# Twelve-head attention of a language-model tower: from turns of two halves to phases over three pairs, with biases as a 97th weight row

## Chip, core and metric

One NeuronCore of one Trainium2 chip. The metric is the device time of the kernel in microseconds (us). A core has five engines that run side by side and meet at semaphores: TensorE (PE; its weight loads are PEld), VectorE (DVE), ScalarE (ACT), GpSimd (POOL) and SyncE (SP).

## What is computed

4096 tokens (32 rows of 128) of width 192 go through an embedding and five blocks. The change is in the fourth: a transformer layer's attention with twelve heads of 16 (over the 128 tokens of a row), and the routing for the mixture of experts that follows. Cut to what matters:

```
qkv  = ln(x) @ in_proj_w.T + in_proj_b          # ln(x) * g + b, width 192
att  = softmax(q @ k.T / 4)  per head, 12 heads, 128 x 128
y    = ln(x) + (att @ v) @ out_proj_w.T + out_proj_b
z    = ln(y)
p    = softmax(ln2(z) @ router_w.T + router_b)  # 8 experts, the best 2 taken
```

The kernel keeps z as rows to send, adds y to its residual, and gives every token two places in the list of rows per expert.

## The kernel before

32 token tiles stay in the SBUF tile resid. The attention block works on **pairs** of tiles (M = 2, 256 tokens), 16 in all; even pairs belong to stream p0 with PSUM banks 0 to 3, odd ones to stream p1 with banks 4 to 7. All engines run the same order, written as generators that `alternate` takes turn by turn; every `yield` is a place where the other generator goes on. `in_turns_routed` (L915) puts `first` of one pair beside `second` of the pair before it in the other stream.

- `first` (`vector_m_1`, `tensor_m_1`, `scalar_m_1`): statistics and normalised rows (DVE L1845 to L1861, the root on POOL L1047), turning (PE L966), features for q and k (24 matmul records at L1007), values (16 at L1000), scores (L1987, 24 records for a tile), row maxima (DVE L1839), which are turned (PE L2036) and put into spare rows of the queries (DVE L1880), scores once more with keys and queries exchanged (L1987), exponentials (ACT L2107), the product with the values (PE L2000).
- `second` (`vector_m_2` and so on): turned back (PE L2008), division (DVE L1888, L1889), turning (L966), output projection (L1000), sum and statistics (DVE L1893, L1019 to L1024), root (POOL L1047), rows of the router (DVE L1030), residual (DVE L1898), turning, router logits (PE L2066).
- `picked` and `placed` run inside the `first` of the stream's next pair: the two best experts by 11 small dependent DVE instructions, running counts, positions by two matmuls (PE L2074, L2075), row numbers; `send` (POOL L1973, L1977) scatters the rows.

An fp32 matmul stands in the profile as two records. `ch.step(ins)` makes DVE wait for its own instruction before the next. The biases of values, output projection and router are added by DVE (L1870, L1861, L1900) from tiles that hold them on all 128 partitions.

Of the kernel before, what the change touches and what calls it, by code (L numbers as in the profile page):

```python
# [16 lines left out]
P = 128  # L17
# [78 lines left out]
def tower(nc, a, out):  # L96

    with ExitStack() as ctx:
# [687 lines left out]
        m_rb, m_rank = W.take(E), W.take(G * E)  # L786
        mb_v, mb_o, mb_qk = W.take(D), W.take(D), W.take(6)
# [51 lines left out]
        for dst, name in ((lw_1b, "L1_attn_w1"), (lw_2b, "L1_attn_w2")):  # L839
# [5 lines left out]
            (mw_r[0:C], halves("L1_ffn_router_w")), (m_rb, rows("L1_ffn_router_b")), (m_rank, AP["rank"]),  # L845
            (mb_v, AP["L1_ffn_in_proj_b"][2 * D:3 * D].partition_broadcast(P)), (mb_o, rows("L1_ffn_out_proj_b")),
# [69 lines left out]
        def in_turns_routed(eng, first, second, routed, over=lambda: None, at_start=lambda: ()):  # L916

            p0, p1 = streams
            alternate(first(0, p0, False), iter(at_start()))
            over()  # L920
            alternate(first(0, p1, False), second(0, p0, False))
            alternate(first(1, p0, True), second(0, p1, False))
# [5 lines left out]
            alternate(first(NG - 1, p1, True), second(NG - 1, p0, True))  # L928
            alternate(second(NG - 1, p1, True), routed(NG, p0))
            over()  # L930
            alternate(routed(NG, p1))
            over()
# [382 lines left out]
        def pool_rest(pool):  # L1315
# [7 lines left out]
            in_turns_routed(pool, lambda g, a, prev: pool_m_1(pool, g, a, m_signals(a), prev),  # L1323
                            lambda g, a, prev: pool_m_2(pool, g, a, m_signals(a), prev),
                            lambda g, a: pool_routed(pool, g, a, m_signals(a)), at_start=lambda: pool_m_pads(pool))
            pool_x(pool)

        def tensor_rest(pe):
# [10 lines left out]
            in_turns_routed(pe, lambda g, a, prev: tensor_m_1(pe, g, a, m_signals(a), prev),  # L1339
                            lambda g, a, prev: tensor_m_2(pe, g, a, m_signals(a), prev),  # L1340
                            lambda g, a: tensor_routed(pe, g, a, m_signals(a)))
            tensor_x(pe)

        def scalar_rest(act):
# [10 lines left out]
            in_turns_routed(act, lambda g, a, prev: scalar_m_1(act, g, a, m_signals(a), prev),  # L1355
                            lambda g, a, prev: scalar_m_2(act, g, a, m_signals(a), prev),
                            lambda g, a: scalar_routed(act, g, a, m_signals(a)))
# [101 lines left out]
        def pool_m_pads(pool):  # L1459

            yield
# [8 lines left out]

        def vector_m_padded(v):

            v.wait_ge(s_pad, 6)
            yield
# [327 lines left out]
        for a in streams:  # L1802
# [4 lines left out]
            a.m_den = take(M * H, M)  # L1807

# [11 lines left out]
        def m_signals(a):  # L1820

            s = Own()
            s.var, s.root, s.x, s.xT_p, s.xT, s.qk_p, s.qk, s.v_p, s.v, s.scores, s.rowmax, s.top_p, s.topped, \
                s.scoresT, s.exp, s.oT_p, s.oT, s.pv_p, s.out, s.T2_p, s.T2, s.proj_p, s.ffn_in, s.T3_p, s.T3, \
                s.router_p, s.r_lg, s.r_eg, s.r_sel, s.r_pos_p, s.r_pos, s.r_dst = a.sems[0:32]
            return s

        def vector_m(v, ch):
            in_turns_routed(v, lambda g, a, prev: vector_m_1(v, ch, g, a, m_signals(a), prev),
                            lambda g, a, prev: vector_m_2(v, ch, g, a, m_signals(a), prev),  # L1830
# [11 lines left out]
        def vector_m_1(v, ch, g, a, f, prev):  # L1842

            for i in range(M):
                ins = nc.vector.bn_stats(a.st[:, i, :], tiles_of(g, a)[:, i, :])  # L1845
# [660 lines left out]
```

## Time and profile before

| | |
|---|---|
| median of 3 runs | 2083.55 us (2078.67 to 2085.76) |
| the profiled execution, span | 2106.3 us |
| its attention block (DVE's first instruction at 1217.2 to the next block's first turned rows at 1718.1) | 501 us |
| mean granted TensorE clock, whole span | 0.822 |
| PE, DVE, ACT, POOL busy | 77%, 62%, 46%, 19% of the span |

The page gives one profiled execution. Its first part sums each engine's busy time over the whole span; its second cuts the span into 40 slices of 52.7 us, of which slices 24 to 32 are the attention block. The granted clock has two levels, 0.5 (1.2 GHz) and 1.0 (2.4 GHz); a digit in between is a mix over time.

### The profile page before, as it was taken

How to read it: one execution, taken by the hardware profiler on the slowest of the kernel's cores; microseconds unless marked ns; L12 is line 12 of the kernel's file. 1: busy time of each engine (PE TensorE's matmuls, PEld its weight loads, DVE VectorE, ACT ScalarE, POOL GpSimd, SP SyncE). 2: the span in 40 equal slices, each digit the busy share in tenths (PEclk: the TensorE clock that was granted, in tenths of full speed). 3: DMA queues.
4: the chain of work that ended last, by engine and by line, in shares of the span. 5: the costliest groups of instructions: out<-in, count | busy, mean ns of one | idle time of the engine just before them, and what ended most of it. 6: DMA issues, size and time to landing. Idle time of an engine off the chain costs nothing.

```text
span 2106.3 us, 35471 instructions
## 1 busy us (share of the span) xinstructions
PE 1611.5 (77%) x12060; PEld 1159.8 (55%) x12060; DVE 1312.3 (62%) x4361; ACT 979.3 (46%) x2773; POOL 400.4 (19%) x494
## 2 busy tenths in 40 slices
PE   0166764968888578888888768888888759999996
PEld 0032223855665355555555456666676647777775
DVE  7898885878888677877788536555555532122221
ACT  1366998933444445554555323333333324443442
POOL 7302331000000100000000001222212223333332
PEclk9975555578888689999999878777777769999998
DMA  3000001079910000000000000000000037777775
GB/s 71 15 1 1 1 1 20 3 141 193 188 20 0 1 1 0 0 0 0 0 0 0 1 25 13 24 23 23 23 15 19 23 96 179 185 175 181 177 176 133
DMA packets 136262, 112.99 MB, mean 54 GB/s; under 512 B 29417, under 2 KB 128457, under 8 KB 136137
## 3 DMA queue, kind: packets, MB, share of 16 engines
q1 hardware_dynamic: 119320, 91.70, 18.4%
q0 software_dynamic: 16864, 20.33, 5.0%
q8 instruction: 40, 0.66, 0.1%
q14 instruction: 38, 0.30, 0.1%
HBM read 69.19 MB, written 45.94 MB: 55 GB/s over the span
## 4 chain that ended last, share of the span: by engine, by line
PE 52%; DVE 27%; ACT 14%; issue 4%; POOL 1%; DVEq 0%; DMA 0%; another core or an unknown queue 0%; SPq 0%; ACTq 0%; POOLq 0%
ACT bank L716 8%; PE bank L2322 8%; PE bank L1007 6%; PE bank L2307 5%; PE bank L2311 3%; PE bank L1987 3%; PE bank L966 3%; PE bank L1217 2%; PE bank L1665 2%; PE bank L1000 2%; PE bank L2000 2%; DVE WK L1839 1%; DVE WK L1581 1%; DVE R L1581 1%; DVE R L1839 1%
## 5 line engine op out<-in xcount | busy, mean ns | idle before, releaser
L1047 POOL TENSOR_TENSOR WK<-WK,mhalf 128x2 f32<-128x2 f32 (+1 forms) x96 | 77.9, 812 | 882.4 <-DVE WK L1505 328.4
L2359 ACT ACTIVATE R<-bank,R 128x256 f32<-128x256 f32 x234 | 98.2, 471 | 216.9 <-PE bank L2311 216.9
L2211 DVE SCALAR_TENSOR_TENSOR WK<-bank,R,WK 128x192 f32<-128x192 f32 x78 | 28.9, 413 | 262.8 <-PE bank L2322 262.8
L716 ACT ACTIVATE bank<-bank,nbias,sc 128x128 f32<-128x128 f32 x384 | 168.9, 991 | 22.6 <-POOL nbias L528 22.6
L1007 PE MATMUL bank<-WK,R 96*128 96x256 f32 x576 | 162.9, 429 | 17.0 <-ACT WK L973 11.0
L2240 POOL DMA_INDIRECT moe_sum<-WK x78 | 121.5, 1557 | 257.4 <-DVE WK L2211 196.4
L2322 PE MATMUL bank<-R 128*128 128x192 f32 x936 | 169.1, 331 | 0.0
L716 ACT ACTIVATION_READ_ACCUMULATOR bank<-bank,nbias,sc 128x1 f32 x384 | 163.0, 766 | 0.0
L2322 PEld LDWEIGHTS bank<-R 128*128 128x128 f32 x936 | 150.1, 190 | 13.3 <-issue 13.3
L1007 PEld LDWEIGHTS bank<-WK,R 96*128 96x128 f32 x576 | 116.2, 213 | 41.9 <-ACT WK L973 15.4
L2307 PE MATMUL bank<-R 128*128 128x256 f32 x468 | 125.2, 390 | 1.1 <-ACT R L2350 1.1
L1987 PE MATMUL bank<-WK 32*128 32x128 f32 x1536 | 84.4, 367 | 35.4 <-DVE R L1839 13.0
L610 PE MATMUL bank<-R 32*128 32x128 bf16 x384 | 62.7, 299 | 60.0 <-ACT bank L716 57.1
L966 PE MATMUL bank<-ident,WK 128*96 128x128 f32 x320 | 66.4, 345 | 44.3 <-DVE WK L1030 27.7
L1987 PEld LDWEIGHTS bank<-WK 32*128 32x128 f32 x1536 | 69.2, 255 | 50.5 <-DVE R L1839 15.3
L2307 PEld LDWEIGHTS bank<-R 128*128 128x128 f32 x468 | 84.0, 191 | 20.9 <-issue 13.3
L610 PEld LDWEIGHTS bank<-R 32*128 32x128 bf16 x384 | 29.4, 118 | 118.7 <-ACT bank L716 106.6
L1665 PE MATMUL bank<-WK,R 128*128 128x256 f32 x256 | 75.6, 420 | 15.0 <-ACT WK L993 15.0
L433 DVE TENSOR_REDUCE neg_all<-bank 128x3 f32<-128x384 f32 x128 | 69.4, 554 | 27.4 <-PE bank L610 25.2
L559 PE MATMUL bank<-R,wq 96*128 96x512 bf16 x192 | 79.3, 542 | 4.6 <-DVE WK L407 2.7
L2311 PE MATMUL bank<-R 64*128 64x256 f32 x468 | 82.7, 430 | 0.0
L1000 PE MATMUL bank<-R,WK 96*128 96x192 f32 x384 | 76.4, 343 | 2.9 <-ACT WK L973 1.4
(494 smaller groups left out, 3886.4 us busy)
## 6 DMA issues: line engine op xcount, KB each, us to landing
moe_rows_in<-zeros SPq DMA_DIRECT2D x1, 25026.0 KB, 138.7
R<-in_L_ffn_w SPq DMA_DIRECT2D x39, 576.0 KB
R<-in_L_ffn_w SPq DMA_DIRECT2D x39, 384.0 KB
R<-moe_rows_in SPq DMA_DIRECT2D x39, 194.0 KB, 4.6
R<-in_L_ffn_w SPq DMA_DIRECT2D x78, 96.0 KB
R<-in_L_ffn_b SPq DMA_DIRECT2D x39, 96.0 KB
moe_sum<-resid POOLq DMA_DIRECT2D x16, 192.0 KB
moe_sum<-WK POOLq DMA_INDIRECT x78, 5.9
```

The source lines that it names most:

```text
L610: mm = nc.tensor.matmul(bank[u % 4][:, k * P:(k + 1) * P], qk[32 * j:32 * j + 32, k, i * P:(i + 1) * P], qk[32 * j:32 * j + 32, 3 + k, i * ...
L716: ins = nc.scalar.activation(s, s, ACT.Exp, bias=nbias[:, u, k:k + 1], scale=col(SS), accum_out=units(sum_all, g, u)[:, k:k + 1])
L966: mm = nc.tensor.transpose(a.bank[b][0:C, c * NM + i * P:c * NM + (i + 1) * P], src[:, i, c * C:(c + 1) * C], ident[:, :])
L1000: mm = nc.tensor.matmul(a.bank[b][:, i * D:(i + 1) * D], a.xT[0:C, c, i * P:(i + 1) * P], w[0:C, c, :], start=(c == 0), stop=(c == 1))
L1007: mm = nc.tensor.matmul(out, w[0:C, c, m], a.xT[0:C, c, :], start=(c == 0), stop=(c == 1))
L1665: nc.tensor.matmul(a.bank[c][:, out], wa[:, c * P:(c + 1) * P], a.xT[:, 0, :], start=True, stop=False)
L1987: mm = nc.tensor.matmul(a.bank[j][:, k * P:(k + 1) * P], x, y, start=True, stop=True)
L2240: pool.indirect_dma_start(out=acc, out_offset=bass.IndirectOffsetOnAxis(ap=x_id[k % B3][:, t:t + 1].bitcast(U32), axis=0), in_=x_y[k % B3] ...
L2307: nc.tensor.matmul(bank[b + n][:, 0:NR], xw_1a[h][:, q * P:(q + 1) * P], x_T[h][:, 0, :], start=True, stop=False)
L2311: mm = nc.tensor.matmul(bank[b + n][:, 0:NR], xw_1b[h][s, p * P:(p + 1) * P], x_T[h][s, 1, :], start=False, stop=True)
L2322: mm = nc.tensor.matmul(bank[4 + t][:, 0:D], x_hid[f][:, t * P:(t + 1) * P], xw_2[h][:, f, :], start=(p == 0 and n == 0), stop=(p == PAIRS ...
L2359: ins = nc.scalar.activation(x_hid[q], bank[(0, 2, 0)[p] + n][:, 0:NR], ACT.Gelu, bias=xb_1[h][:, q:q + 1])
```

## The change

- `in_phases` takes the place of `in_turns_routed`. A phase works on up to five things: S, the pair whose scores are made; T, the pair before it, from its product with the values to its normalised rows; N, the pair after it, turned and multiplied to q, k and v (in T's stream); L, the pair two after S, whose statistics and normalised rows are made; R, the pair two before S, which is routed. There are 16 phases with an S, and two more that empty the line.
- PE's, DVE's, ACT's and POOL's orders inside a phase are written out. On DVE `weave` puts an instruction of a filler (the picking of R, the statistics of L) behind each of the main one; `mark` and `need` wait for a step only where its result is used.
- The biases of values, output projection and router are row 97 of the weights (partition 96), against a row of ones in `xT` and in a new tile `m_tT`. DVE's three additions go; ACT copies the values out of PSUM (`take_values`) and makes the base of the sum (`base`). T's turned rows go to `m_tT` and no longer over `xT`.
- N's features use banks 0 and 1 of T's stream, T's and R's turned rows bank 2, projection and logits bank 3.
- POOL's memsets (`pool_m_pads`) stand ahead of its first root, and DVE waits for them before its first statistics.

```diff
-            alternate(first(0, p0, False), iter(at_start()))
...
+            phase((0, p0), None, (0, p1), (1, p0), None)
+            phase((0, p1), (0, p0), (1, p0), (1, p1), None)
             over()
             with eng.Fori(1, NG - 1) as g:
-                alternate(first(g, p1, True), second(g, p0, True))
-                alternate(first(g + 1, p0, True), second(g, p1, True))
+                phase((g, p0), (g - 1, p1), (g, p1), (g + 1, p0), (g - 1, p0))
+                phase((g, p1), (g, p0), (g + 1, p0), (g + 1, p1), (g - 1, p1))
                 over()
...
+            phase(None, (NG - 1, p1), None, None, (NG - 1, p0))
+            phase(None, None, None, None, (NG - 1, p1))
...
+            def phase(S, T_, N_, L_, R):
+                r = picked(*R) if R else iter(())
+                l = normed_twice(*L_) if L_ else iter(())
+                if S:
+                    run(row_tops(*S, 0))
+                if R:
+                    run(logits(*R))
+                if S:
+                    weave(row_tops(*S, 1), r)
+                if T_:
+                    weave(divided(*T_), r)
+                if S:
+                    weave(tops_into_queries(*S), r)
+                if T_:
+                    weave(attended(*T_), r, l)
+                run(r)
+                run(l)
+                if T_:
+                    run(routed_rows(*T_))
+                p = placed(*R, other(R[1]).bank[2][:, 0:M * E]) if R else iter(())
+                if L_:
+                    weave(rows_of_pair(*L_), p)
+                run(p)
...
+            def with_bias(x, w, out):
+                for i in range(M):
+                    n = w.shape[2]
+                    nc.tensor.matmul(out[:, i * n:(i + 1) * n], x[0:C + 1, 0, i * P:(i + 1) * P], w[0:C + 1, 0, :],
+                                     start=True, stop=False)
+                    mm = nc.tensor.matmul(out[:, i * n:(i + 1) * n], x[0:C, 1, i * P:(i + 1) * P], w[0:C, 1, :],
+                                          start=False, stop=True)
+                return mm
...
+                if S:
+                    g, a = S
+                    f = m_signals(a)
+                    pe.wait_ge(f.qk, per(g, 4, 4))
+                    scores(g, a, 0, f.scores, False)
+                if R:
+                    gr, c = R
+                    fr = m_signals(c)
+                    if T_:
+                        pe.wait_ge(m_signals(T_[1]).exp, per(T_[0], 4 * M, 8))
+                    pe.wait_ge(fr.ffn_in, per(gr, 2, 1))
+                    turn(other(c), c.xr, 2, fr.T3_p)
+                if T_:
+                    gt, b = T_
+                    ft = m_signals(b)
+                    times_v(*T_, 0)
+                    times_v(*T_, 1)
+                if R:
+                    pe.wait_ge(fr.T3, per(gr, 1, 1))
+                    with_bias(c.m_tT, mw_r, other(c).bank[3]).then_inc(fr.router_p, 1)
+                if S:
+                    pe.wait_ge(f.rowmax, per(g, 4 * M, 4))
+                    scores(g, a, 1, f.scores, False)
+                if N_:
+                    gn, n = N_
+                    fn = m_signals(n)
+                    pe.wait_ge(fn.x, per(gn, 1, 1))
+                    if T_:
+                        pe.wait_ge(ft.oT, per(gt, M, 1))
+                    turn(n, n.hs, 0, fn.xT_p)
...
+                if T_:
+                    pe.wait_ge(ft.out, per(gt, M, M))
+                    turn(b, b.m_ao, 2, ft.T2_p)
+                if S:
+                    tops_turned(*S, 0)
+                    tops_turned(*S, 1)
+                if T_:
+                    pe.wait_ge(ft.T2, per(gt, 1, 1))
+                    with_bias(b.m_tT, mw_o, b.bank[3]).then_inc(ft.proj_p, 1)
+                if N_:
+                    features(n, 0)
+                if S:
+                    pe.wait_ge(f.topped, per(g, M, M))
+                    scores(g, a, 0, f.scoresT, True)
+                if N_:
+                    pe.wait_ge(fn.qk, per(gn, 4, 1))
+                    features(n, 2)
+                    pe.wait_ge(fn.qk, per(gn, 4, 2))
+                    with_bias(n.xT, mw_v, n.bank[0]).then_inc(fn.v_p, 1)
+                if R:
+                    positions(*R, other(c).bank[2][:, 0:M * E])
+                if S:
+                    pe.wait_ge(f.exp, per(g, 4 * M, 4))
+                    scores(g, a, 1, f.scoresT, True)
+                if T_:
+                    pe.wait_ge(ft.var, per(gt, 1, 1))
+                if R:
+                    pe.wait_ge(fr.r_pos, per(gr, 1, 1))
```

How the order of instructions moves, as the two programs issue them (an ISA or REGISTER_ALU row is a wait that stands by itself or an address; counts are instructions). First PE in the loop, from the scores of a pair's first tile to its second scores. Before, with L966 turning, L2036 the turned row maxima, L1000 a product with the values' or the projection's weights and L2066 the router:

```order
L1987 MATMUL bank<-WK 128x128 x12
L1000 MATMUL bank<-R,WK 128x192 x4
L2031 REGISTER_ALU
L1987 MATMUL bank<-WK 128x128 x12
L2034 REGISTER_ALU
L2036 MATMUL bank<-ident,R 128x128 x6
L966 MATMUL bank<-ident,WK 96x128 x4
L1987 MATMUL bank<-WK 128x128 x12
L2066 MATMUL bank<-R,WK 128x8 x4
```

In the changed kernel (L2101 the scores, L967 turning, L2124 turned back, L1008 features, L2108 the turned maxima):

```order
L2101 MATMUL bank<-WK 128x128 x12
L2176 REGISTER_ALU
L967 MATMUL bank<-ident,WK 96x128 x4
L2124 MATMUL bank<-ident,R 128x128 x3
L2122 REGISTER_ALU
L2124 MATMUL bank<-ident,R 128x128 x3
L1008 MATMUL bank<-WK,R 128x256 x4
L967 MATMUL bank<-ident,R 96x128 x4
L2106 REGISTER_ALU
L2108 MATMUL bank<-ident,WK 128x128 x3
```

Between the scores of the second tile and the turned maxima, where PE had no other instruction, there now stand two turnings, the turned-back tiles and a third of the next pair's features.

Second, DVE where a routed pair's experts are picked. Before:

```order
L1888 RECIPROCAL WK<-bank 128x12
L1889 TENSOR_TENSOR WK<-bank,WK 128x192
L1914 TENSOR_REDUCE R<-R 128x2
L1915 TENSOR_TENSOR R<-R 128x16
L1916 TENSOR_TENSOR R<-R 128x16
L1917 TENSOR_REDUCE R<-R 128x2
L1918 TENSOR_TENSOR R<-R 128x16
L1920 SCALAR_TENSOR_TENSOR R<-R 128x16
```

In the changed kernel (L1883 the row maxima, L1902 and L1906 the division, the rest the picking):

```order
L1883 TENSOR_REDUCE WK<-bank 128x3
L1953 TENSOR_TENSOR R<-R 128x16
L1883 TENSOR_REDUCE WK<-bank 128x3
L1956 TENSOR_TENSOR R<-R 128x16
L1883 TENSOR_REDUCE WK<-bank 128x3
L1960 TENSOR_REDUCE R<-R 128x2
L1901 ISA
L1902 RECIPROCAL WK<-bank 128x12
L1963 TENSOR_TENSOR R<-R 128x16
L1901 REGISTER_ALU
```

Each step of the picking now has an instruction of another chain between it and the step that it needs.

## Rows read from the trace of the kernel before

**Rows 1.** The page: busy time by engine over the whole span.

```profile
PE 1611.5 (77%) x12060; PEld 1159.8 (55%) x12060; DVE 1312.3 (62%) x4361; ACT 979.3 (46%) x2773; POOL 400.4 (19%) x494
```

**Rows 2.** Windows: length; busy PE, PEld, DVE, ACT, POOL; clock. Earlier block, attention, one turn.

```profile
900.00:1200.00 300.00, 243.83 (x2006) 162.52 (x2004) 237.33 (x734) 151.33 (x400) 24.26 (x30) 0.98 0.00 0
1217.00:1718.00 501.00, 390.41 (x3524) 316.73 (x3524) 274.01 (x1077) 168.51 (x386) 109.00 (x135) 0.72 0.07 22
1458.00:1516.00 58.00, 48.15 (x442) 39.22 (x441) 33.22 (x132) 20.84 (x49) 13.26 (x16) 0.74 0.06 20
```

**Rows 3.** Timeline, PE at the upper clock: start, length, group, idle before.

```profile
1400.05 1.97 PE L1007 MATMUL bank<-WK,R 96*128 96x256 f32 x8
...
1401.86 1.46 PE L1000 MATMUL bank<-R,WK 96*128 96x192 f32 x8
...
1403.16 0.60 PE L966 MATMUL bank<-ident,WK 128*96 128x128 f32 x4
...
1408.10 0.95 PE L1987 MATMUL bank<-WK 32*128 32x128 f32 x24 [1.52 <-DVE WK L1839]
```

**Rows 4.** Timeline, PE at the lower clock.

```profile
1395.13 0.83 PE L2008 MATMUL bank<-ident,R 128*128 128x128 f32 x3
...
1411.92 0.90 PE L2036 MATMUL bank<-ident,WK 128*128 128x128 f32 x3 [0.49 <-DVE WK L1839]
...
1413.60 1.67 PE L1987 MATMUL bank<-WK 32*128 32x128 f32 x24
...
1415.20 1.88 PE L2066 MATMUL bank<-R,WK 96*128 96x8 f32 x8
...
1422.57 1.51 PE L2000 MATMUL bank<-R,WK 128*32 128x128 f32 x24
```

**Rows 5.** PE's busy time and clock in pieces of 1.5 us.

```profile
1394.00:1395.50 1.50, 1.50 (x26) 0.50 0.00 0
1395.50:1397.00 1.50, 1.50 (x9) 0.91 0.00 0
...
1406.00:1407.50 1.50, 0.58 (x4) 1.00 0.19 66
1407.50:1409.00 1.50, 0.90 (x24) 1.00 0.39 134
1409.00:1410.50 1.50, 0.05 (x4) 0.64 0.19 64
```

**Rows 6.** Timeline, DVE, POOL and ACT.

```profile
1398.67 0.17 DVE L1918 TENSOR_TENSOR R<-R 128x16 f32<-128x16 f32 x1
1398.88 0.17 DVE L1923 COPY R<-routing 128x8 f32<-128x8 f32 x1
1398.96 0.17 DVE L1924 TENSOR_TENSOR R<-R 128x16 f32<-128x16 f32 x1
...
1409.91 1.95 DVE L1839 TENSOR_REDUCE WK<-bank 128x3 f32<-128x384 f32 x4
1410.14 0.72 POOL L1047 TENSOR_TENSOR WK<-WK,mhalf 128x2 f32<-128x2 f32 x1 [1.95 <-DVE WK L1024]
...
1411.78 0.66 DVE L1030 TENSOR_SCALAR WK<-WK 128x192 f32<-128x192 f32 x2
...
1413.71 1.01 ACT L977 ACTIVATE WK<-bank,R 96x256 f32<-96x256 f32 x2 [0.30 <-PE bank L966]
...
1415.33 1.64 ACT L2107 ACTIVATE R<-bank 128x384 f32<-128x384 f32 x4 [0.61 <-PE bank L1987]
...
1419.78 1.01 POOL L1047 TENSOR_TENSOR WK<-WK,mhalf 128x4 f32<-128x4 f32 x1 [8.92 <-DVE WK L1851]
```

**Rows 7.** The block's first scores, its last send, the next block's first turned rows.

```profile
L1987 PE MATMUL bank<-WK x1536: 270/416/578, 1236.0 to 1679.0; 32*128 32x128 f32 x192
...
1707.62 0.18 POOL L1970 TENSOR_TENSOR still<-mhalf 128x1 f32<-128x1 f32 x1 [5.14 <-DVE R L1944]
...
1718.08 0.47 PE L2291 MATMUL bank<-ident,R 128*128 128x128 f32 x1 [9.64 <-DVE R L2217]
```

More of the change, by code:

```diff
@@ L1459, in pool_m_pads @@
         def pool_m_pads(pool):
-            yield
             for a in streams:
@@ new lines, in pool_m, with root_of_rows, root_of_attended, send @@
+        def pool_m(pool):
+            def root_of_rows(g, a):
+                f = m_signals(a)
+                pool.wait_ge(f.n_var, per(g, 1, 1))
+                nc.gpsimd.tensor_tensor(a.m_rs, a.m_ve, mhalf[:, 0:2 * M], ALU.pow).then_inc(f.n_root, 1)
+            def root_of_attended(g, a, sent):
+                f = m_signals(a)
+                if sent:
+                    pool.wait_ge(x_sc[a.n], per(g, 80, 0))
+                pool.wait_ge(f.var, per(g, 1, 1))
+                nc.gpsimd.tensor_tensor(a.rs[:, 0:M], a.ve[:, 0:M], mhalf[:, 0:M], ALU.pow).then_inc(f.root, 1)
+            def send(g, a):
+                f = m_signals(a)
+                pool.wait_ge(f.r_dst, per(g, 1, 1))
+                nc.gpsimd.tensor_tensor(still[:, 2 + a.n:3 + a.n], mhalf[:, 0:1], mhalf[:, 0:1], ALU.add)
+                for i in range(M):
+                    for n in range(2):
+                        pool.indirect_dma_start(out=xs, out_offset=bass.IndirectOffsetOnAxis(
+                            ap=a.r_ati[:, n, i:i + 1].bitcast(U32), axis=0), in_=a.r_row[:, i, n, :], in_offset=None
+                        ).then_inc(x_sc[a.n], 16)
+                pair = g * 2 + a.n
+                pool.dma_start(acc[bass.ds(pair * (M * P), M * P), :].rearrange("(t p) d -> p t d", p=P),
+                               tiles(resid[:, bass.ds(pair * (M * D), M * D)])).then_inc(x_sc[a.n], 16)
+            def phase(S, T_, N_, L_, R):
+                if L_:
+                    root_of_rows(*L_)
+                if T_:
+                    root_of_attended(*T_, sent=T_[1].n == 0 and not (isinstance(T_[0], int) and T_[0] == 0))
+                if R:
+                    send(*R)
+                    if R[1].n == 1:
+                        pool.wait_ge(x_sc[1], per(R[0], 80, 80))
+            pool.wait_ge(s_zero, 16)
+            pool_m_pads(pool)
+            root_of_rows(0, streams[0])
+            root_of_rows(0, streams[1])
+            in_phases(phase, pool)
@@ new lines, in tensor_m, with scores, tops_turned @@
+        def tensor_m(pe):
+            def scores(g, a, i, done, turned):
+                for k in range(3):
+                    for j in range(4):
+                        sl = slice(32 * j, 32 * j + 32)
+                        q, kk = a.m_qk[sl, k, i * P:(i + 1) * P], a.m_qk[sl, 3 + k, i * P:(i + 1) * P]
+                        x, y = (kk, q) if turned else (q, kk)
+                        mm = nc.tensor.matmul(a.bank[j][:, k * P:(k + 1) * P], x, y, start=True, stop=True)
+                mm.then_inc(done, 1)
+            def tops_turned(g, a, i):
+                f = m_signals(a)
```

617 lines of the change are left out of this document (338 added, 279 removed).

## Prediction

> **What bounds the kernel now.** I read first the page, then the windows, then the timeline of one turn. The page shows PE as the busiest engine, 77% of the span, ahead of DVE with 62% [rows 1]; that is an average over stages, so the attention block is read by itself. In a turn of two pairs (58.0 us) PE is busy 48.15 us, DVE 33.22, ACT 20.84, and the clock is 0.74 [rows 2]. So a pair takes 29.0 us, and PE sits idle in 4.9 of them. PE is the bound, but by way of its clock. The reader should see this in the pieces of 1.5 us: PE waits for the row maxima, is busy in 0.58, 0.90 and 0.05 us of three pieces, and during the third the clock falls to its lower level [rows 5]. What it does next runs at half speed: 24 score records take 1.67 us and not 0.95 [rows 3, 4]. The clock comes back at about 1395.6, after PE had been without a gap for a while [rows 5]. Every pair pays this once. The block before this one has PE busy 81% of the time with gaps spread out, and a clock of 0.98 [rows 2]: it is the long gap, and not the share, that costs.
>
> **PE's work for a pair.** Lengths overlap by about 0.15 us with the next group, so I count from start to start. At the upper level: features, three groups of 8 records, 1.81 each (1400.05 to 1401.86) is 5.4; values and projection 1.30 each (to 1403.16), 2.6; scores four times 0.88 (0.95 less 0.07), 3.5; three turnings at 0.5, 1.5 [rows 3]. The rest stands only at the lower level, and I take 0.55 of it, as the scores show (0.88 against 1.60): router 1.83 to 1.0, two products with the values 1.44 to 0.8 each, turned back and turned maxima 0.7 to 0.35 or 0.4 each [rows 4], two matmuls for positions 0.4. The sum is 1.0 + 1.6 + 1.5 + 0.4 with the former 13.0: **17.5 us**. As a test: 24.1 us busy times 0.74 is 17.8 [rows 2]. At the lower level throughout the same work is about 33 us.
>
> **Part 1, the order in phases.** I lay out one phase with R, T, S, N, L at the upper clock, t = 0 where PE ends S's first scores. Between engines I add 0.05 to 0.15 us.
> - PE waits until ACT has made the last pair's exponentials (4 in 1.64 [rows 6], begun when PE ended the scores before), until 0.9. Turning of R 1.4, both products 3.1.
> - ACT has still to copy rows to send and make `base` (0.95 and 0.65), until 2.5, and takes R's turned rows until 3.5 (1.01 [rows 6]). PE's router waits for it, from 3.55 to 4.5; second scores 5.4. DVE's first row maxima need 1.95 [rows 6], from 0.1: hidden, where PE stood still for 1.52 before [rows 3].
> - N's turning 5.9, turned back 6.6, wait for ACT's copy until 7.1, features 8.9. DVE: maxima of the second tile with four fillers until 7.9, division until 9.3. PE waits 0.4; turning of T 9.85, turned maxima 10.7, projection 12.0, features 13.8, scores of the first tile exchanged 14.7, features 16.5, values 17.8, positions 18.0, exchanged scores of the second 18.9, next S's first 19.8.
> - DVE: maxima into the queries until 11.5, from 12.2 the sum and the statistics with two fillers each until 14.7. POOL then makes two roots one behind the other, 1.01 and 0.72 [rows 6], until 16.6; rows of the router (0.66 [rows 6]) and residual until 17.8; L's rows and R's places until about 19.7. DVE is ready as PE ends the next scores, and has 1.9 us in hand before PE needs the maxima.
>
> So a phase is 19.8 us; a loop turn costs a few tenths, and DVE's slack is thin: I take **20.5 us**. No idle stretch of PE is longer than 0.9 us, against the 4 us with 1.5 busy before the clock falls now [rows 5], so it stays at the upper level; that is what most of the gain hangs on. Either half alone would give little: at clock 0.74 even a gapless PE needs 23.8.
>
> **Part 2, DVE.** Its 16.6 us a pair [rows 2] lose the three bias additions (0.56, 0.62, 0.17) and two of four normalisations (0.62), and gain one small instruction. A dependent small step now starts 0.21 after the last, an independent one 0.08 (1398.67, 1398.88, 1398.96 [rows 6]); some 19 picking steps as fillers win up to 0.12 each, 2 us. DVE falls to 13 to 15 us, below PE. This is no gain by itself, but it is what lets the walk above close.
>
> **Part 3, ACT and the bias row.** ACT gains the values' copy (0.6) and `base` (0.65), 10.4 to 11.8 us a pair. PE's matmuls take 97 instead of 96 rows at the same count; between nothing and one row in 96 (0.03 us of 3.6) I take nothing. Fewer broadcast loads: they land before the block, nothing. POOL's sends keep their number; they begin at a phase's end and have half a phase until POOL's next root.
>
> **Part 4, ends.** First scores come 18.8 us after the start [rows 2, 7]. POOL's memsets now precede DVE's statistics (3 us), and values precede the scores, so 21. The first phase has no T and one wait for the maxima in the open, partly at the lower clock: 18 (13 at the upper, 23 at the lower). Fifteen phases follow at 20.5, 307.5. The two that empty the line are chains of DVE and PE: 15 and 10.5, and from the last places to the next block stays 10.5 (1707.6 to 1718.1 [rows 7]). Sum 21 + 18 + 307.5 + 15 + 10.5 + 10.5 = 382.5 us, against 501 now: **118.5 us less**. The profiled execution would go from 2106.3 to 1988. It lies 1.1% above the median of the runs; taking the gain as it is from the median gives 2083.6 - 118.5 = **1965 us**.
>
> **Rivals.**
> - *Handshakes add up.* PE, DVE, ACT and POOL each have a place within 0.5 us of the path; one more late step (POOL's two roots in a row, a copy behind exponentials) goes round all four. For it: DVE's slack is nil at the phase's end. Against: the waits now seen are mostly 0.05 to 0.3. A phase of 23.5 gives 75 + 352.5 = 427.5, 73.5 less, 2010 us. Chance 0.16.
> - *The clock still falls once a phase.* From the router (weights for 8 columns, little streaming) through two turnings to the wait at 7.1, PE streams full matmuls for only 0.9 of 3.5 us. If that counts as idleness, the clock stays 0.74, a phase is 17.6 / 0.74 + 2.2 = 26 us, and the block 75 + 390 = 465, 36 less: 2048 us. Against: at 1395.13 PE was turning tiles back and the clock rose right behind it [rows 4, 5]. By this rule, the trace disagrees: the Trainium skill, TensorE: Matmul & The Clock Gate, PE-mode transpose, says that transposes do not count as PE being busy for the clock. Chance 0.13.
> - *Slower: the clock never rises.* At the start it is at the lower level, and rises only after PE had been dense. If the small gaps of each phase always spoil that, all phases run at the lower level, 33 and a gap, 34 us: 44 + 510 + 45 = 599, 98 more, 2182 us. The point is whether PE ever runs gapless; in the stretch from projection to values it has 5.8 us without a wait at the upper level and 11 at the lower, longer than the busy stretch ahead of the rise now. Chance 0.03.
> - *The order changes, the pace does not* (DVE's in-order waits tie pairs together as before, 28 to 29 us a phase): no change. Chance 0.02.
>
> **How the numbers follow.** The forecast has 0.66 and holds for phases from 19.3 to 22 us: 1947 to 1988. The range goes down to 1938 for ends shorter than mine, and up to 2010 to take in the first rival, leaving out 0.18. A measurement of this kernel tells 0.3% (6 us) from no change. Faster 0.66 + 0.16 + 0.13 = 0.95, same 0.02, slower 0.03.
>
> **What the changed profile would show.** The attention block about 380 us long; a turn of two pairs 41 us; clock above 0.95 and PE busy 85 to 90% in it; no wait of PE for row maxima of the first tile; waits of 0.4 to 0.9 us at R's turning, N's features and T's turning; DVE 26 to 30 us busy in a turn; other blocks unchanged. I am wrong if the clock there is under 0.9 (second or third rival), or if it is 1.0 and PE idles over 4 us a phase, with DVE waiting for POOL or ACT (first).

## The result and the profile after

The changed kernel takes 1980.49 us (median of 4 runs, 1978.83 to 1982.94) where the kernel before, beside it, takes 2083.24 (4 runs, 2078.67 to 2085.76): a ratio of 0.9504, with a 95% interval of 0.9491 to 0.9517. That is 102.8 us less; 118.5 were forecast, and 1965 us, in a range from 1938 to 2010. The profiled execution spans 1977.9 us. The profile of before spans 2106.3, so the two profiles are 128.4 us apart. Both facts need an explanation: the gain between the profiles is larger than forecast, and the gain between the medians smaller.

The page of the changed kernel, which answers to [rows 1]:

```profile
span 1977.9 us, 35529 instructions
...
PE 1524.7 (77%) x12060; PEld 1101.4 (56%) x12060; DVE 1250.6 (63%) x4284; ACT 995.7 (50%) x2837; POOL 399.9 (20%) x494
```

PE runs as many matmuls as before in 87 us less of busy time: the same work at a higher clock. Windows of the changed kernel, in the columns of [rows 2]: the block before, the attention block, and two phases (four sends' starts show a phase to be 20.0 us, so this is what a turn of 58.0 was).

```profile
900.00:1200.00 300.00, 243.15 (x2002) 162.25 (x2002) 236.74 (x733) 152.10 (x402) 24.25 (x30) 0.98 0.00 0
1216.00:1596.00 380.00, 308.60 (x3539) 261.37 (x3540) 212.44 (x1005) 187.45 (x455) 108.92 (x135) 0.91 0.10 34
1313.70:1353.80 40.10, 35.67 (x440) 30.68 (x440) 25.15 (x122) 22.89 (x58) 13.41 (x17) 1.00 0.09 30
```

The block before is unchanged. In two phases PE is busy 35.67 us of 40.10 and the clock is 1.00; before, it was 48.15 of 58.00 at 0.74. PE's work for a pair is 17.8 us, against the 17.5 counted in the prediction and 24.1 before. PE at the places of the walk (timeline of the changed kernel; in brackets the idle time before and what ended it); it answers to [rows 3] and [rows 4]:

```profile
1331.81 0.94 PE L2101 MATMUL bank<-WK 32*128 32x128 f32 x24
...
1333.75 0.64 PE L967 MATMUL bank<-ident,WK 128*96 128x128 f32 x4 [1.00 <-ACT R L2264]
1334.32 1.52 PE L2116 MATMUL bank<-R,WK 128*32 128x128 f32 x48
...
1336.33 0.39 PE L2131 MATMUL bank<-R 97*128 97x8 f32 x2 [0.49 <-ACT R L978]
...
1337.32 0.95 PE L2101 MATMUL bank<-WK 32*128 32x128 f32 x24
...
1339.94 1.99 PE L1008 MATMUL bank<-WK,R 96*128 96x256 f32 x8 [0.45 <-ACT WK L978]
...
1343.34 0.59 PE L2131 MATMUL bank<-R,WK 97*128 97x192 f32 x2 [0.31 <-ACT WK L974]
...
1353.82 0.64 PE L967 MATMUL bank<-ident,WK 128*96 128x128 f32 x4 [0.56 <-ACT R L2264]
```

The reader can lay these beside the walk. With t = 0 at 1332.75, where the first scores end, R's turning starts at 1.00 (forecast 0.9), the router at 3.58 (3.55), second scores at 4.57 (4.5), features at 7.19 (7.1), projection at 10.59 (10.7). From turning to turning is 20.07. PE's idle time is in waits for ACT of 1.0 us or less, and 0.33 us at the loop's branch. The widest wait, 1.00 us, lies in the window of two phases above, whose clock is 1.00 throughout. The pieces of 1.5 us around the next two (0.49 us at the router, 0.45 at the features) can be laid beside [rows 5], now with no fall:

```profile
1336.00:1337.50 1.50, 1.17 (x12) 1.15 (x16) 0.08 (x1) 1.03 (x3) 1.20 (x2) 1.00 0.34 119
1337.50:1339.00 1.50, 1.50 (x31) 1.38 (x31) 0.94 (x5) 0.34 (x2) 1.25 (x2) 1.00 0.24 80
1339.00:1340.50 1.50, 1.05 (x8) 0.76 (x7) 1.50 (x6) 0.89 (x2) 0.00 (x0) 1.00 0.39 131
```

DVE and POOL, answering to [rows 6]: the picking stands between the maxima and between the divisions, and the two roots follow one another as the walk had them.

```profile
1339.35 0.17 DVE L1953 TENSOR_TENSOR R<-R 128x16 f32<-128x16 f32 x1
1339.43 0.55 DVE L1883 TENSOR_REDUCE R<-bank 128x3 f32<-128x384 f32 x1
1339.90 0.17 DVE L1956 TENSOR_TENSOR R<-R 128x16 f32<-128x16 f32 x1
...
1347.86 1.04 POOL L2055 TENSOR_TENSOR WK<-WK,mhalf 128x4 f32<-128x4 f32 x1 [9.11 <-DVE WK L1860]
...
1348.89 0.69 POOL L2062 TENSOR_TENSOR WK<-WK,mhalf 128x2 f32<-128x2 f32 x1
...
1349.61 0.67 DVE L1031 TENSOR_SCALAR WK<-WK 128x192 f32<-128x192 f32 x2 [1.48 <-POOL WK L2062]
```

The ends of the block, answering to [rows 7] (scores, start of the last send, next block's first turned rows):

```profile
L2101 PE MATMUL bank<-WK x1536: 270/270/575, 1235.5 to 1549.8; 32*128 32x128 f32 x192
...
1579.03 0.18 POOL L2067 TENSOR_TENSOR still<-mhalf 128x1 f32<-128x1 f32 x1 [3.65 <-DVE R L2014]
...
1589.32 0.48 PE L2490 MATMUL bank<-ident,R 128*128 128x128 f32 x1 [9.41 <-DVE R L2416]
```

From the first scores to the next block's turned rows, called **the stretch** from here on, is 353.8 us; the prediction's sum without its first term is 361.5. In the profile of before the stretch is 482.1 (1236.0 to 1718.1). The difference, 128.3 us, is nearly all of the 128.4 that separate the two profiles.

### The profile page after: what moved, and what is told of

The parts are those of the page before. It is cut to its first block, busy times and chain, and to the rows that moved or that the text cites. A ratio compares the mean times of both kernels' runs of the same rounds, so it can differ in the third digit from the quotient of the medians.

```text
span 1977.9 us, 35529 instructions
## 1 busy us (share of the span) xinstructions
PE 1524.7 (77%) x12060; PEld 1101.4 (56%) x12060; DVE 1250.6 (63%) x4284; ACT 995.7 (50%) x2837; POOL 399.9 (20%) x494
## 4 chain that ended last, share of the span: by engine, by line
PE 51%; DVE 23%; ACT 18%; issue 5%; POOL 1%; DMA 0%; DVEq 0%; ACTq 0%; POOLq 0%; SPq 0%
ACT bank L716 9%; PE bank L2521 8%; PE bank L1008 6%; PE bank L2506 6%; PE bank L2510 4%; PE bank L2101 2%; PE bank L1218 2%; PE bank L1654 2%; PE bank L967 2%; PE bank L2131 2%; DVE WK L1570 2%; DVE R L1570 2%; PE bank L2133 1%; PE bank L1657 1%; PE bank L640 1%
## 5 line engine op out<-in xcount | busy, mean ns | idle before, releaser
L1048 POOL TENSOR_TENSOR WK<-WK,mhalf 128x2 f32<-128x2 f32 (+1 forms) x64 | 50.4, 788 | 666.5 <-DVE WK L1494 328.4
L1008 PE MATMUL bank<-WK,R 96*128 96x256 f32 x576 | 163.3, 424 | 24.4 <-ACT WK L978 13.4
L1008 PEld LDWEIGHTS bank<-WK,R 96*128 96x128 f32 x576 | 111.4, 205 | 52.7 <-ACT WK L978 20.1
L967 PE MATMUL bank<-ident,WK 128*96 128x128 f32 x288 | 49.2, 297 | 53.7 <-DVE WK L1031 24.4
L2242 ACT ACTIVATE WK<-bank,R 128x256 f32<-128x256 f32 x96 | 40.4, 472 | 93.5 <-PE bank L1008 93.5
L433 DVE TENSOR_REDUCE neg_all<-bank 128x3 f32<-128x384 f32 x128 | 69.5, 554 | 27.4 <-PE bank L610 25.2
L528 POOL TENSOR_SCALAR nbias<-neg_all,sc 128x3 f32<-128x3 f32 x128 | 38.6, 301 | 198.3 <-DVE neg_all L433 198.0
```

Of the source, the lines that this page charges most:

```text
L967: mm = nc.tensor.transpose(a.bank[b][0:C, c * NM + i * P:c * NM + (i + 1) * P], src[:, i, c * C:(c + 1) * C], ident[:, :])
L1008: mm = nc.tensor.matmul(out, w[0:C, c, m], a.xT[0:C, c, :], start=(c == 0), stop=(c == 1))
```

## The experiments

Twelve kernels ran, in three groups of four. Each group ran on one core of a chip of its own, with the kernel before beside it. Its median was 2085.16 us on the first chip, 2101.84 on the second and 2108.05 on the third. The second and the third chip are slower than the one of the first runs, which matters below. In the table the stretch is in us and the last column is the mean clock between 1312.8 and 1492.8 us.

| kernel | chip | us | ratio to before | stretch | phase or pair, us | clock, 1312.8 to 1492.8 |
|---|---|---|---|---|---|---|
| before, once more | 1 | 2085.87 | 1.0006 | 458.3 | 27.3 | 0.74 |
| tops at once | 1 | 2048.59 | 0.9825 | 421.4 | 23.8, later 24.7 and 26.5 | 0.91 |
| tops after turnings | 1 | 2015.31 | 0.9669 | 387.2 | 22.2 | 1.00 |
| no weave | 1 | 1998.19 | 0.9583 | 370.9 | 19.9 to 25.9 | 0.91 |
| before, filled | 2 | 2082.47 | 0.9898 | 455.2 | 27.3 | 0.87 |
| roots swapped | 2 | 2008.30 | 0.9558 | 381.2 | 22.2 | 0.96 |
| bias on DVE | 2 | 2018.63 | 0.9607 | 393.0 | 21.8 to 23.6 | 0.94 |
| three moves | 2 | 2039.22 | 0.9706 | 410.0 | 24.1 to 26.0 | 0.86 |
| changed kernel, once more | 3 | 2011.31 | 0.9544 | 384.9 | 22.3 | 0.96 |
| roots swapped, once more | 3 | 2012.03 | 0.9543 | 384.6 | 22.2 | 0.96 |
| three moves, once more | 3 | 2045.75 | 0.9707 | 420.1 | 24.7 and 26.4 | 0.84 |
| three moves, late sends | 3 | 1967.69 | 0.9334 | 341.3 | 18.8 | 1.00 |

### Before, once more

No edit.

> The kernel before, unchanged. The profile of it that the prediction used had a span of 2106.3 us, 22.7 above the median of its runs, while the profiled run of the changed kernel lies within 2 us of its median. Theory: in the timed runs the attention block of the kernel before goes at another mix of the two clock levels than in that one profile (a turn of two pairs under 58.0 us, clock in the block above 0.72), so that a fresh profile has a span of 2077 to 2086, with the block at about 480 us instead of 501 and every other block as it was. Rival: the missing 22 us lie outside the attention block, or in the profiling itself, and a fresh profile has a turn of 58.0 us again with a block of 501.

2085.87 us, ratio 0.9997 to 1.0015. Its profile spans 2082.0, and not 2106.3: the stretch is 458.3 and not 482.1, a pair 27.3 and not 29.0. So the profile read ahead of the prediction was of an execution some 24 us longer than this one, and 23.8 of them lie in the stretch. Another mix of the two clock levels, which was expected as the cause, is not what differs in the loop: the clock between 1312.8 and 1492.8 is 0.74 in both. Against this profile the changed kernel's stretch is 104.5 us shorter, close to the 102.8 of the medians. Where most of a pair's 1.7 us come from, one row of each timeline shows. DVE starting the row maxima in the profile of before, when PE had ended the scores at 1405.08 (1404.13 and 0.95 long):

```profile
1406.09 1.95 DVE L1839 TENSOR_REDUCE WK<-bank 128x3 f32<-128x384 f32 x4 [2.11 <-PE bank L1987]
```

and in the fresh one, with the scores' end at 1395.96:

```profile
1395.01 0.95 PE L1987 MATMUL bank<-WK 32*128 32x128 f32 x24 [0.37 <-DVE WK L1870]
...
1396.02 1.95 DVE L1839 TENSOR_REDUCE WK<-bank 128x3 f32<-128x384 f32 x4 [1.15 <-PE bank L1987]
```

In the old profile DVE stands still for 1.0 us with its input ready, 3.9 us after POOL has begun a pair's sends. In the fresh one it starts at once. PE's gap behind it is 1.52 us in the one and 0.57 in the other. This goes on through the whole block: in the old profile these maxima start 0.06 us after the scores in the first two pairs, beside which POOL sends nothing yet, and 1.0 us or more after them in the fourteen that follow (1.0 to 1.2 in all but the last); in the fresh profile it is 0.06 us in all sixteen.

### Tops at once: the gap back in PE's order

The turned maxima again right behind the second scores, with all the rest of the change kept:

```diff
                     scores(g, a, 1, f.scores, False)
+                    tops_turned(*S, 0)
+                    tops_turned(*S, 1)
                 if N_:
...
-                if S:
-                    tops_turned(*S, 0)
-                    tops_turned(*S, 1)
```

> The changed kernel, but PE turns the row maxima right behind the second tile's scores, with nothing in between: PE stands idle for some 2 us once a phase until DVE has the maxima. Theory (the long gap costs the clock, as it did before the change): the clock falls once in nearly every phase, a phase goes from 20.0 to 25 or 26 us, the kernel to 2050 to 2075 us. Rival (a gap costs only itself): the clock stays at its upper level, a phase is 21.5 to 22.5 us, the kernel 2003 to 2018 us.

2048.59 us, 0.9810 to 0.9840: two thirds of the gain are gone. A phase of 23.8 us and this time lie just under the 25 to 26 and the 2050 to 2075 of the theory, and far above the rival's 2003 to 2018. PE's windows around the gap in one phase:

```profile
1331.40:1332.90 1.50, 0.95 (x25) 0.76 (x24) 0.82 (x4) 0.22 (x1) 1.46 (x2) 1.00 0.35 120
1332.90:1334.40 1.50, 0.55 (x3) 0.31 (x3) 1.50 (x7) 0.00 (x0) 0.00 (x0) 1.00 0.42 140
1334.40:1335.90 1.50, 1.23 (x8) 1.21 (x9) 0.29 (x2) 0.00 (x0) 0.00 (x0) 0.76 0.00 0
1335.90:1337.40 1.50, 1.50 (x8) 1.27 (x7) 0.35 (x3) 1.02 (x2) 0.00 (x0) 0.50 0.00 0
```

PE is busy 0.95 and 0.55 of two pieces, and in the next the clock falls, for 3.4 us in each phase; after 1480 it is 6.8 to 10.2 us and the phases grow from 23.8 to 24.7 and 26.5. Of the parts of the change that were put back one at a time, the place of this turning is the largest.

### Tops after turnings: the gap filled with turnings alone

As before, but twenty extra turnings of N's rows (into a bank that N's own turning then writes over) stand ahead of the turned maxima. This kernel does more work than the changed one.

```diff
+                    for _ in range(5):
+                        for h in range(2):
+                            for i in range(M):
+                                nc.tensor.transpose(n.bank[0][0:C, h * NM + i * P:h * NM + (i + 1) * P],
+                                                    n.hs[:, i, h * C:(h + 1) * C], ident[:, :])
                     turn(n, n.hs, 0, fn.xT_p)
+                if S:
+                    tops_turned(*S, 0)
+                    tops_turned(*S, 1)
...
-                if S:
-                    tops_turned(*S, 0)
-                    tops_turned(*S, 1)
```

> As tops_at_once, but the wait for the row maxima is filled by turning the next pair's rows five times more than needed (20 transposes with the same result, 2.5 us). Theory that transposes count as PE being busy for the clock: the clock stays at its upper level, a phase is 21.5 to 22.5 us, the kernel 2003 to 2020 us. Rival, that transposes do not count: the clock falls as in tops_at_once, a phase is 25 us or more, the kernel 2050 us or more.

2015.31 us, 0.9654 to 0.9684. The clock in the loop is 1.00 and the phase 22.2, which is 20.0 and the 2.2 of the twenty turnings. PE from the second scores on, and the windows of that stretch:

```profile
1325.33 0.95 PE L2101 MATMUL bank<-WK 32*128 32x128 f32 x24
1326.21 2.39 PE L2182 MATMUL bank<-ident,WK 128*96 128x128 f32 x20
1328.44 0.60 PE L967 MATMUL bank<-ident,WK 128*96 128x128 f32 x4
```

```profile
1326.00:1328.00 2.00, 2.00 (x28) 1.88 (x21) 1.65 (x7) 0.07 (x1) 0.79 (x2) 1.00 0.43 148
1328.00:1330.00 2.00, 2.00 (x21) 2.00 (x20) 0.62 (x3) 0.92 (x2) 0.00 (x0) 1.00 0.00 0
```

Where PE idled and the clock fell, 2.2 us of nothing but turnings keep it at its upper level. By this, the trace disagrees with what the prediction cited from the Trainium skill, TensorE: Matmul & The Clock Gate, PE-mode transpose. Doing 2.2 us of useless work takes 33 us off the kernel.

### No weave

DVE's fillers run in a block behind the main steps, at the same places:

```diff
-                for _ in main:
-                    for x in fill:
-                        next(x, None)
+                steps = sum(1 for _ in main)
+                for x in fill:
+                    for _ in range(steps):
+                        next(x, None)
```

> The changed kernel with the same DVE instructions between the same groups, but the filler's steps stand behind the main ones in a block and not one behind each. Theory: each filler step then waits for the one before it, 0.1 us each, 18 steps, so DVE needs up to 2 us more a phase; DVE's division then comes late for PE's turning, and a phase grows by 0.5 to 2 us, the kernel to 1988 to 2010 us. Rival: PE is the bound and DVE has room, a phase grows by less than 0.2 us, the kernel stays within 4 us of 1980.5.

1998.19 us, 0.9568 to 0.9597: 18 us more than the changed kernel. That is in the range of the theory, but the loss did not come the way the theory had it. Most phases stay at 19.9 to 20.3, so DVE's slack does cover the dependent steps. The loss comes in single phases of 21.2 to 25.9, in which the clock falls for 3.4 to 13.7 us. Behind the loop's branch PE stands for 1.20 us without waiting for a semaphore, where the changed kernel has 0.33:

```profile
1374.37 0.95 PE L2102 MATMUL bank<-WK 32*128 32x128 f32 x24
1376.52 0.95 PE L2102 MATMUL bank<-WK 32*128 32x128 f32 x24 [1.20 <-issue]
```

The loop's pauses alone come to 7.2 us in the stretch (6 pauses), against 1.6 (5 pauses) in the changed kernel. What share of the rest is the missing weave's, and why the pause is longer, one kernel cannot tell; it stays open.

### Before, filled

Twelve turnings at each of the two waits for the maxima in the kernel before (again more work, and nothing of it is used):

```diff
+            for _ in range(12):
+                nc.tensor.transpose(streams[1 - a.n].bank[1][:, 0:P], ident[:, :], ident[:, :])
             pe.wait_ge(f.rowmax, per(g, 4 * M, 4))
             scores(pe, g, a, f, 1, f.scores, False)
+            for _ in range(12):
...
```

> The kernel before with 12 transposes of the identity into a bank that nobody reads ahead of the second tile's scores, and 12 more behind them, that is where PE waits for the row maxima: 24 transposes, 3 us of extra PE work a pair at the upper level, and nothing else changed. Theory (the kernel before lost most of its time to the clock, and only by that idle stretch): the clock stays at its upper level in most of the block, a pair goes from 27.3 us to 22.5 to 24.5, and the kernel gets faster by extra work, 2020 to 2045 us. Rival: the lower level has other causes too (the router's short matmuls, the turnings), the clock in the block stays under 0.8, and the kernel takes 2085 to 2120 us.

2082.47 us against 2101.84 on this chip, 0.9880 to 0.9917. A window of one pair:

```profile
1360.00:1387.30 27.30, 24.28 (x246) 19.94 (x245) 16.81 (x68) 10.33 (x24) 6.64 (x8) 0.87 0.06 22
```

The clock is 0.87, against 0.74 in both profiles of the kernel before. A pair takes 27.3 us; unfilled it took 27.3 on the first chip and 29.0 in the profile read ahead of the prediction, in which DVE starts late as it does here (1.0 to 1.1 us in all pairs but one of those that have sends beside them). So a better clock, bought with 24 turnings a pair, gives the old order 1% net, 19 us. Both expectations missed: the theory had 2020 to 2045 us, the rival a clock under 0.8 and 2085 or more. That a pair is bound there by its chain through DVE, ACT and PE as much as by PE's pace, and that the gain so needs both the filled gap and an order with other work beside each wait, is the likely reading, but argued: the turnings' own time and the late starts are in the same number.

### Roots swapped, bias on DVE, three moves

Three edits of the changed kernel on the second chip. First, POOL makes T's root ahead of L's:

```diff
+                if T_:
+                    root_of_attended(*T_, ...
                 if L_:
                     root_of_rows(*L_)
-                if T_:
-                    root_of_attended(*T_, ...
                 if R:
```

> The changed kernel, with POOL making the root of the attended rows ahead of the root for the rows two pairs on. It shortens DVE's way to the router's rows by 1.0 us a phase. Theory (PE is the bound of a phase of 20.0 us, DVE has room there): no difference beyond 4 us from 1980.5, rather none. Rival (DVE's chain through the two roots is on the path, as the forecast's walk had it nearly): a phase is 0.3 to 1.0 us shorter, 1965 to 1976 us.

2008.30 us, 0.9545 to 0.9571, where about 1980 or less was expected. Second, matmuls of 96 rows, and the biases of values, projection and router added by DVE again:

```diff
-                    nc.tensor.matmul(out[:, i * n:(i + 1) * n], x[0:C + 1, 0, i * P:(i + 1) * P], w[0:C + 1, 0, :],
+                    nc.tensor.matmul(out[:, i * n:(i + 1) * n], x[0:C, 0, i * P:(i + 1) * P], w[0:C, 0, :],
...
+                k = mark(nc.vector.tensor_tensor(a.x, a.x, wide(mb_o), ALU.add))
+                need(k)
```

> The changed kernel with the biases off the weights (96 rows again) and back on DVE: values are taken and biased by DVE at the end of its phase, the output bias is one more addition in the sum, the router's another. DVE gains 1.35 us a phase, ACT loses 0.55. Theory (DVE's slack ahead of the row maxima, 1.9 us by the forecast and 1.0 us less by the trace's start of the maxima, takes it nearly all, and the values come later): a phase is 0.3 to 1.2 us longer, 1985 to 2000 us. Rival (the 97th row is what the gain hangs on): over 2 us a phase, over 2010 us.

2018.63 us, 0.9594 to 0.9621, 10 us above the swapped roots on the same chip. Third, three moves meant to take PE's remaining waits away: the swapped roots; PE's product of the first tile ahead of R's turning, and second scores and N's turning ahead of the router; ACT's rows to send and `base` early in the phase:

```diff
+                if T_:
...
+                    times_v(*T_, 0)
                 if R:
...
                     turn(other(c), c.xr, 2, fr.T3_p)
                 if T_:
...
-                    times_v(*T_, 0)
                     times_v(*T_, 1)
-                if R:
...
-                    with_bias(c.m_tT, mw_r, other(c).bank[3]).then_inc(fr.router_p, 1)
                 if S:
...
                     scores(g, a, 1, f.scores, False)
...
                     turn(n, n.hs, 0, fn.xT_p)
+                if R:
...
+                    with_bias(c.m_tT, mw_r, other(c).bank[3]).then_inc(fr.router_p, 1)
```

> The changed kernel in another order: PE multiplies the first tile by its values ahead of R's turning, does the second tile's scores and N's turning ahead of the router; ACT copies R's rows to send and makes the base one phase later, behind the products; DVE picks behind the third of the second tile's maxima; POOL's roots are swapped. By the trace of the changed kernel PE waits 1.0 us for exponentials, 0.49 for R's turned rows and 0.45 for N's turned rows in a phase of 20.0. Theory (these three waits are the path): a phase of 18.3 to 19.0 us, 1955 to 1968 us. Rival (the waits come back elsewhere, at the division or at DVE's chain, or the idle time adds up and the clock falls): 19.6 us or more, 1975 us or more.

2039.22 us, 0.9693 to 0.9719, where 1955 to 1968 was the theory: the version in which PE waits least for other engines is the slowest of the three. All three show something that the first profile of the changed kernel does not: pauses of PE of 0.2 to 0.9 us with no semaphore behind them, 35, 37 and 60 in the stretch, all within 6.2 us of the start of a pair's sends but for those at the loop's branch. This called the expectations of this group into question, since they had been worked out from phases of 20.0 us; it left open whether the chip or the altered orders bring the pauses. Hence the last group.

### The same kernels with the changed one beside them

> The changed kernel, unaltered, once more. Theory (the pauses of PE without a semaphore beside POOL's sends, seen with the two roots swapped, and the slower pace of the kernel before in that group of runs, belong to the core they ran on): 1978 to 1983 us where the kernel before takes 2083 to 2087, and some 20 us more, with 30 such pauses in nine phases, where the kernel before takes 2100 or more. Rival (they belong to the altered orders): none of them here on either core, phase 20.0 us.

2011.31 us, 0.9530 to 0.9558: the unaltered kernel takes 31 us more on this chip than in its first runs (some 20 were expected), with phases of 22.3 us. PE's and POOL's rows in one phase (two pieces of the timeline):

```profile
1360.78 1.05 POOL L2070 DMA_INDIRECT moe_rows_in<-R  x1 [0.17 <-issue]
...
1362.05 1.29 PE L2116 MATMUL bank<-R 128*32 128x128 f32 x38
...
1363.61 0.45 PE L2116 MATMUL bank<-R 128*32 128x128 f32 x4 [0.27 <-issue]
1364.38 0.39 PE L2116 MATMUL bank<-R 128*32 128x128 f32 x3 [0.32 <-issue]
...
1365.12 0.42 PE L2116 MATMUL bank<-R 128*32 128x128 f32 x3 [0.35 <-issue]
...
1365.62 0.78 POOL L2074 DMA_DIRECT2D moe_sum<-resid  x1
1366.55 0.29 PE L2133 MATMUL bank<-R,WK 96*128 96x8 f32 x2 [0.69 <-issue]
```

The product with the values was one group of 48 records in 1.52 us; here it breaks into pieces, about 0.75 us from pause to pause. Between 1313 and 1495 PE has 26 pauses of 11.2 us together, against 4 of 1.3 in the first profile, which are those at the loop's branch. So the altered orders do not bring the pauses; they go with where the kernel ran. Chip, core and hour changed together from group to group, so which of these it is was not separated; below, "a chip with pauses" means no more than this.

> POOL's two roots in the other order, once more, now beside the changed kernel on the same core. Theory (the pauses belong to the core): within 4 us of the changed kernel. Rival (the pauses come with this order): 8 us or more above it, phases of 22 us with the clock falling in every second one.

2012.03 us, 0.9528 to 0.9559: no different from the changed kernel. Swapping the roots is worth nothing, on a chip with pauses at least. It also makes "bias on DVE" readable: its ratio of 0.9607 stands against 0.9544 and 0.9558 of kernels that have the bias row, so there the row, with the additions that it takes off DVE, is worth 10 to 13 us.

> The three small moves together, once more, now beside the changed kernel on the same core. Theory (the pauses belong to the core): where there are none, a phase of 18.3 to 19.0 us at the upper clock and 15 to 25 us less than the changed kernel; where there are, the clock falls again and it is slower than it. Rival (a denser order brings the pauses by itself): slower than the changed kernel by 20 us or more on any core.

2045.75 us, 0.9693 to 0.9721, 34 us more than the changed kernel. On a chip with pauses theory and rival both allow that; since this kernel never ran on a chip without them, what it does there is open. Why a denser order is slower here, four windows show (PE's busy time is the first, the clock the third column from the end):

```profile
1342.00:1344.00 2.00, 1.96 (x36) 1.39 (x36) 0.99 (x3) 0.56 (x2) 1.39 (x3) 1.00 0.14 50
1344.00:1346.00 2.00, 1.33 (x13) 0.94 (x14) 0.00 (x0) 0.83 (x2) 1.70 (x2) 1.00 0.29 99
1346.00:1348.00 2.00, 1.29 (x10) 0.74 (x7) 0.34 (x1) 0.75 (x2) 0.99 (x2) 0.91 0.37 126
1348.00:1350.00 2.00, 2.00 (x12) 1.99 (x11) 1.15 (x3) 1.58 (x4) 0.00 (x0) 0.50 0.06 22
```

Pauses in a row make PE idle for a third of 4 us, and the clock falls at their end, as it did behind the old wait. The moves bring the second tile's scores, 24 records in 0.95 us, to where the sends are: in this phase they start at 1343.35, 2.3 us after the sends, and take until 1347.6.

The last kernel keeps the three moves and lets POOL begin the sends later:

```diff
                 if L_:
                     root_of_rows(*L_)
+                if R and L_:
+                    pool.wait_ge(m_signals(L_[1]).xT, per(L_[0], 1, 1))
                 if R:
```

> The three small moves together, and POOL begins the sends of a routed pair only when the next pair's turned rows are there, so that they run beside other work of PE. Theory (the pauses come where the sends meet PE's short matmuls): pauses gone or under a quarter of those without the wait, 1955 to 1975 us on a core that has them, and within 4 us of the version without the wait on a core that has none. Rival (the pauses follow the sends wherever they are): as many pauses, within 6 us of the version without the wait.

1967.69 us, 0.9321 to 0.9347, on the slowest of the three chips: 43.6 us less than the changed kernel beside it, 78 less than without this one wait, and the fastest of all. Phases are 18.8 us, the clock 1.00. Rows beside one pair's sends:

```profile
1334.87 0.19 POOL L2076 TENSOR_TENSOR still<-mhalf 128x1 f32<-128x1 f32 x1 [8.30 <-ACT WK L978]
...
1335.78 1.89 PE L1008 MATMUL bank<-WK,R 96*128 96x256 f32 x8
...
1337.71 0.84 ACT L2254 ACTIVATE WK<-bank,R 128x256 f32<-128x256 f32 x2 [1.24 <-issue]
...
1339.08 0.59 PE L2142 MATMUL bank<-R,WK 97*128 97x192 f32 x2 [0.31 <-issue]
...
1340.49 1.89 PE L1008 MATMUL bank<-WK,R 96*128 96x256 f32 x8
```

The pauses have not gone. Between 1313 and 1495 PE has 14 of 4.4 us together, 0.45 us a phase (9.7 phases), against 31 of 11.8, 1.65 a phase (7.1 phases), without the wait. That is 27%, not under a quarter as the theory had it. ACT now has 10 of 1.2 us each and DVE 5 of 1.1, which have slack. PE runs features there, 8 records in 1.9 us, and is hardly touched, and the clock does not fall. What this version gives on a chip without pauses was not tried.

## Why the prediction was right, and where it was off

- **What bounds the kernel** held: the gap behind the scores and the clock that falls after it. Putting the gap back alone cost 68 us ("tops at once"), and 2.2 us of turnings in its place recovered 33 of them. Of the signs that the prediction named, a turn is 40.1 us (forecast 41), with a clock of 1.00 (above 0.95) and PE busy in 89% (85 to 90); DVE is busy 25.2 us in it, a little under the 26 to 30.
- **PE's work** (17.5 us a pair) came out at 17.8, and **the phase** (walk 19.8, taken 20.5) at 20.0. The 0.7 added for loop turns and thin slack was 0.5 too much, 7.5 us over fifteen phases. The stretch was forecast at 361.5 and is 353.8 us long.
- **The step that failed** is the last of the sum: "taking the gain as it is from the median". The gain was counted against a profile whose stretch took 482.1 us, and taken off runs whose stretch took about 458. Sized by the old profile the stretch saves 128.3 us, by the fresh one 104.5. The 1.1% between profile and median was noted and put down to nothing; it lay in the very stretch that the change rewrites. With 458.3 in the place of 482.1 the same working gives 94.7 less, 1989 us. So the forecast's nearness to the measured time owes something to luck: its gain was 23.8 us too large by the profile it was counted on and 7.7 too small by its walk, and the two partly cancel in the 15.7 us by which it missed.
- **Part 2** (DVE's weaving is no gain by itself) is half borne out: without it most phases take 19.9 to 20.3 us, and nearly all of the 18 us are lost in the others. That it is what lets the walk close was not shown.
- **Part 3** put the bias row at nothing in the sum. On a chip without pauses it was not tried alone; on the second chip it is worth 10 to 13 us, together with DVE's additions.
- **Rivals.** Handshakes did not add up: DVE's wait for the two roots, 1.48 us a phase, is not followed by any wait of PE for DVE, and swapping the roots changed nothing. The clock did not fall once a phase in the profile of the first runs, so the second rival fell there; on the chips with pauses it falls for 3.4 us in about every second phase, by a mechanism that no rival named. The other two, a clock that never rises and an order that keeps its pace, were never seen: between 1312.8 and 1492.8 the clock is 0.84 or more in every changed version. That either half alone would give little was tested for the clock: 1% net in "before, filled", on a chip with pauses.

## What to carry to other kernels

When a profile's own time stands apart from the median by as much as a few per cent of the stretch that is to change, find out first where in the program the excess lies; a gain counted on a profile belongs to that profile. A gap in TensorE's order that costs the clock of the work behind it is worth filling with any work at hand, provided that the order can use the pace: the same means gave 33 us in the new order and 19 in the old. And where engines pause beside a DMA burst of another engine, the burst is part of the schedule: here it did best beside long instructions, and not beside trains of short ones.

## What the runs showed of the hardware

- On two of three chips engines pause with their inputs ready, for 0.2 to 1.2 us at a time, within some 6 us of the start of POOL's scatters. On the second chip DVE's maxima in "before, filled" start 1.0 us late (0.06 in the first two pairs, which have no sends beside them); on both, PE's products and scores break up, and on the third ACT waits 1.24 us. The old profile of before has DVE's late starts too, and its span of 2106.3 is like that of the slower chips. On the first chip, under the same scatters, none was seen. Groups of about 30 records a microsecond suffer most, groups of 4 hardly. That points to instructions arriving too slowly beside the scatters' traffic, which the profile does not show: argued, not shown. The Trainium skill, Runtime: NRT & Kernel Launch, Instruction fetch mechanics, calls the cost of fetching the next block of instructions mostly hidden, and says that a taken branch whose target is not in the pages at hand stalls until it is fetched. The traces have a pause at the loop's branch (0.33 us at each turn, 1.20 without the weave), but not its cause; if the pauses beside the sends are fetches, two chips disagree with the first part.
- The clock stays up through twenty turnings in a row, and falls after two pieces of 1.5 us with PE busy in 0.95 and 0.55.
- The same program has one pace on one chip and another on the next: 27.3 and (in the old profile, whose chip is not known) 29.0 us a pair before, 20.0 and 22.3 a phase after. Ratios hold better: 0.9504 and 0.9544 for this change.
